# Preparing the next chunk six ticks earlier in a software-pipelined scan, with the logarithm's table change moved along

## The chip, the cores and the metric

One core of a Trainium2 chip runs the whole program in one launch. The metric is device time in microseconds of one execution; the profile is of one such execution. Engines are named as in the profile: PE is TensorE, DVE is VectorE, ACT is ScalarE, POOL is GpSimd, SP issues nearly all transfers.

## What is computed

Sixteen images of 64 channels and 64 x 64 pixels go through two layers (16 x 4096 positions each):

```python
# layer 0
y = leaky(conv3x3(x)); y = leaky(conv3x3(y)); seq = y as (image, 4096, 64)
x, z = split(seq @ in_proj)                       # 128 wide each
x = silu(causal_conv4(x) + b)
dt, B, C = split(x @ x_proj);  delta = softplus(dt @ dt_proj + dt_b)
h = exp(delta * A) * h + (delta * x) * B          # 4096 steps, 128 channels x 16 states
y = (h . C + x * D) * silu(z) @ out_proj
# layer 1, on y as (image, 64, 4096)
channel attention (64 x 64 softmax), spatial attention softmax(q^T k) (4096 x 4096), 1x1 conv, residual
```

softplus is done as max(t, 0) + ln(1 + exp(-|t|)) with a correction of the rounding of the sum, silu by the hyperbolic tangent; so ScalarE needs exp, tanh and ln.

## The kernel before

After the two convolutions (some 540 us), `pipeline` runs everything else as one software pipeline, written out by hand for each engine. Its unit is the *tick* T. An image has 128 ticks; 16 ticks (`GROUPS`) are a *chunk* of 512 positions. In each tick the scan handles one group of 8 channels x 16 states on 128 partitions: VectorE forms `DBU` (L1175, delta x u x B, into a bank) and runs the scan (L1189); ScalarE forms `dA` for the next tick (L1046, exp); GpSimd multiplies by C (L1317). In the same tick TensorE and the others do 1/128 of the attention of the image before: one difference product and one maximum product of the key search (L852, bank to `gains` by ScalarE L982, then VectorE's maximum L1127), four score products (L915, L917), ScalarE's two exponentials into `pr` (L1040), TensorE's products of the tick before with the values (L927) and, every second tick, with ones (L942). Image 0 has no attention beside it; behind the last scan tick, attention runs alone.

On top of that, once per chunk, come two chains, each step tied to r = T mod 16:

- the *preparing chain* of the chunk that comes next (`c = sl + 1`): r 0 `xin` and `z` products (L870), their copies, the first tap `cacc` (L1069); r 1 to 3 three taps on VectorE (L1219); r 4, 5 tanh (L1076, L1079); r 5, 6 gating into `u` and `zs` (L1229, L1234); r 6 the `dt` product (L874), its copy `dtx` (L1023), abs and exp (L1084, L1086), and the load of a later `seqt`; r 7 two VectorE steps; r 8 the logarithm (L1090); r 9 VectorE's `em1`, `dsp` (L1248, L1251) and GpSimd's `usp` (L1330); r 10 the stores of `dsp` and `usp` to `spread_d`, and the `BC` products (L878); r 11 the stores of `bcs`; r 12 the two broadcasts back, `bbc` and `cbc` (L724, L727).
- the *finishing chain* of the chunk that is done (`c = sl - 1`): r 2 the 32 products of `y` (L889), r 3 `ysb` (L1167, VectorE), r 4 the product with `zs` on GpSimd (L1323), r 7 `out` (L884), r 8 to 12 the split into three bfloat16 parts, r 12 `xv`, r 14 `en` and the stores of the parts.

Each engine runs its list in order and waits on semaphores. The SP queue is in order too: in each tick it fetches `lanes` for T + 3 (L736, 512 KB, four slots), behind whatever stores or loads its list has before. Every product uses the next of five banks of a ring (`RING`), and may start when the bank's use five before has been taken away by ScalarE or VectorE (`take_bank`). The order of the ring is the order of `plan` (L232). An `xin`, `z` or `dt` product shifts it by one.

ScalarE's tables: one table serves exp and tanh, another the logarithm. The compiler puts a table load in front of an activation that needs the other one, so twice a chunk.

Of the kernel before, what the change touches and what calls it, by code (L numbers as in the profile page):

```python
# [19 lines left out]
ALU = mybir.AluOpType  # L20
# [40 lines left out]
AHEAD = 3  # L61

# [41 lines left out]
class Span:  # L104
# [89 lines left out]
    def small_uses(self, T):  # L194
# [234 lines left out]
def pipeline(nc, banks, seq_d, scratch, w_in, cw, cb, w_dt_t, w_dt, dt_b, w_bc, a_log, skip,  # L429
# [4 lines left out]
    with ExitStack() as ctx:  # L434
        def sb(name, shape, dt=F32):
            return ctx.enter_context(nc.sbuf_tensor(name, shape, dt))
# [22 lines left out]
        u = sb("u", [P, 2, CHUNK])  # L459
# [22 lines left out]
        energy = sb("energy", [CH, CH])  # L482
# [12 lines left out]
        nmx = sb("nmx", [NT, 3, P])  # L495
        nm3 = sb("nm3", [NT, 3, P], BF16)
# [5 lines left out]
        catt = sb("catt", [CH, CH])  # L502
        cst1 = sb("cst1", [CH, 4])

# [14 lines left out]
        with nc.Block() as block:  # L519
            @block.vector  # L520
            def _(dve):
                nc.vector.memset(wxv[CH:P], 0.0)
                nc.vector.memset(mixw[:], 0.0)
                nc.vector.memset(ones[:], 1.0).then_inc(zeroed, 1)
# [48 lines left out]
        def span(j, images, tail, i):  # L573
# [22 lines left out]

            def bank_of(e):
                return RB[number[e] % RING]
# [16 lines left out]
            for T in range(sched.first, sched.last):  # L615
# [14 lines left out]
                c = sl + 1  # L630
# [7 lines left out]
                if r == 6 and sched.chunk(c + 2):  # L638
                    sched.note(f"seq{c % 2}", c + 2)
                elif T == sched.first == -GROUPS:  # L640
                    sched.note("seq0", 0)
                    sched.note("seq1", 1)
                c = sl - 1
# [26 lines left out]
            with nc.Block() as block:  # L670
                @block.sync
                def _(sp):
# [28 lines left out]
                    for T in range(first, last):  # L701
                        sl, r = T // GROUPS, T % GROUPS
                        c = sl + 1
# [34 lines left out]
                        c = sl - 1  # L738
# [96 lines left out]
                def _(pe):  # L835
# [6 lines left out]
                    def small_use(e):  # L842
# [29 lines left out]
                        elif kind == "dt":  # L872
                            wait(pe, "gated", c)
                            mm = nc.tensor.matmul(bank[:], wdt[:], u[:, c % 2, :], start=True, stop=True)  # L874
                        elif kind == "BC":
                            wait(pe, "gated", c)
                            for j in range(BLOCKS):
                                mm = nc.tensor.matmul(bank[BLOCK * j:BLOCK * (j + 1), 0:P], wbc[:],  # L878
                                                      u[:, c % 2, P * j:P * (j + 1)], start=True, stop=True,
# [92 lines left out]
                def _(act):  # L972
# [54 lines left out]
                    for T in range(first, last):  # L1027
# [36 lines left out]
                        c = sl + 1  # L1064
# [6 lines left out]
                        if sched.chunk(c) and r == 4:  # L1071
# [3 lines left out]
                            taken(act, ("y", c - 2))  # L1075
                            nc.scalar.activation(u[:, c % 2, :], cacc[:], ACT.Tanh).then_inc(S["tanh"], 1)  # L1076
# [14 lines left out]
                        c = sl - 1  # L1091
# [15 lines left out]
                def _(dve):  # L1107
# [52 lines left out]
                    for T in range(first, last):  # L1160
# [3 lines left out]
                        if sched.chunk(c) and r == 3:  # L1164
                            full_wait(dve, ("y", c))
                            full_wait(dve, ("out", c - 1))
                            nc.vector.scalar_tensor_tensor(out=ysb[:], in0=u[:, c % 2, :], scalar=dskip, in1=bank_of(("y", c))[:],  # L1167
# [38 lines left out]
                        c = sl + 1  # L1206
                        if sched.chunk(c):
# [18 lines left out]
                            if r == 5:  # L1226

                                wait(dve, "tanh", c)
                                nc.vector.scalar_tensor_tensor(out=u[:, c % 2, :], in0=u[:, c % 2, :], scalar=1.0,  # L1229
# [23 lines left out]
                        c = sl - 1  # L1253
# [46 lines left out]
                def _(pool):  # L1300
                    for T in range(first, last):
# [23 lines left out]
                        c = sl + 1  # L1325
                        if sched.chunk(c) and r == 9:
# [3 lines left out]
                            nc.gpsimd.tensor_tensor(usp[:], dsp[:], u[:, c % 2, :], ALU.mult).then_inc(S["du_in"], 1)  # L1330
# [44 lines left out]
```

## Time and profile before

| | us |
|---|---|
| three runs | 8232.38, 8223.09, 8398.1; median 8232.38 |
| the profiled execution | 8230.45 |
| its span, first to last instruction | 8228.7 |
| PE, DVE, ACT, POOL busy in the span | 7514.0 (91%), 6835.1 (83%), 5962.8 (72%), 3796.9 (46%) |
| first to last scan | 589 to 7820 |
| an inner chunk with attention (16 ticks) | 56.1 |

The page divides the span in 40 slices: from the fourth on TensorE is at 9 or 8 tenths nearly everywhere, VectorE at 8 or 9, and the DMA engines at 7 or 8 tenths with about 200 GB/s. The granted TensorE clock is full but for a few slices at the start (mean 0.966). So no engine stands out by its share alone, and what counts is the order of the work within a chunk. In the waits, idle time of an engine that isn't the bottleneck costs nothing: GpSimd's 2343 us of waiting for `DBU` is of that kind.

### The profile page before, as it was taken

To read this page: it belongs to the slowest core of one execution; us is meant where nothing else is said; L and a number is where in the kernel's file an instruction comes from. 1 tells how busy PE (TensorE), PEld (TensorE's weight loads), DVE (VectorE), ACT (ScalarE), POOL (GpSimd) and SP (SyncE) were. 2 spreads that over 40 slices of the span, in tenths; PEclk is the share of its full clock that TensorE was granted. 3 is DMA by queue.
4 is the path that set the end of the run, shared out by engine and by line. 5 is a ranking of instruction groups with operands and counts; after the bars stand their busy time and mean duration, and the time that the engine had idled before them with its cause. 6 is when DMAs were issued, how large, how long until landed. Compare 5 with 4: busy or idle time off the path is not lost. (4 is left out here: it accounts for less than half of the span.)

```text
span 8228.7 us, 151814 instructions
## 1 busy us (share of the span) xinstructions
PE 7514.0 (91%) x47106; PEld 2297.2 (28%) x47854; DVE 6835.1 (83%) x11132; ACT 5962.8 (72%) x10582; POOL 3796.9 (46%) x4135
## 2 busy tenths in 40 slices
PE   9962389999999999999989999999999999999998
PEld 2321122222222222222222222222222222222222
DVE  2228898898989889898888889888889898998876
ACT  1124577787878788787878788788878787887765
POOL 0016555555545455555545455555545454555500
PEclk9985699999999999999999999999999999999999
DMA  9838888888787788888877888888888878888710
GB/s 152 134 91 215 219 200 200 204 197 208 193 206 199 197 201 200 200 201 201 198 189 198 199 200 200 199 200 200 202 199 198 205 193 202 201 200 205 191 32 15
DMA packets 886523, 1530.96 MB, mean 186 GB/s; under 512 B 409480, under 2 KB 459472, under 8 KB 885712
## 3 DMA queue, kind: packets, MB, share of 16 engines
q1 hardware_dynamic: 882640, 1520.79, 76.7%
q8 instruction: 381, 6.24, 0.4%
q14 instruction: 430, 3.52, 0.2%
q10 hardware_dynamic: 3072, 0.40, 0.0%
HBM read 1326.69 MB, written 176.95 MB: 183 GB/s over the span
## 5 line engine op out<-in xcount | busy, mean ns | idle before, releaser
L1317 POOL TENSOR_TENSOR hst<-hst,cbc 128x512 f32<-128x512 f32 x2048 | 2620.2, 1279 | 2370.6 <-DVE bank L1175 2343.4
L1189 DVE TENSOR_TENSOR_SCAN hst<-dA,carry,bank 128x512 f32<-128x512 f32 x1792 | 2283.9, 1275 | 4.9 <-DVE bank L1175 0.4
L1040 ACT ACTIVATE pr<-bank 128x512 f32<-128x512 f32 x4096 | 2230.1, 604 | 43.2 <-PE bank L917 41.0
L927 PE MATMUL bank<-pr,vt 128*32 128x512 f32 x16384 | 2193.5, 608 | 0.7 <-ACT pr L1040 0.7
L982 ACT ACTIVATE gains<-bank 128x512 f32<-128x512 f32 x2048 | 1225.2, 598 | 832.7 <-PE bank L852 790.7
L1046 ACT ACTIVATE dA<-lanes,small 128x512 f32<-128x512 f32 x2048 | 1503.8, 734 | 431.8 <-DMA lanes<-spread_d 383.9
L852 PE MATMUL bank<-s1kx,s1q 128*128 128x512 bf16 x4096 | 1581.9, 387 | 133.0 <-DMA s1kx<-kx_d 84.9
L1127 DVE CUSTOM_DVE_ANT_0 gains<-bank,gains 128x512 f32<-128x512 f32 x2048 | 1404.3, 686 | 352.7 <-PE bank L852 333.9
L1175 DVE TENSOR_TENSOR bank<-lanes,bbc 128x512 f32<-128x512 f32 x2048 | 1505.0, 735 | 146.1 <-DMA lanes<-spread_d 65.0
L917 PE MATMUL bank<-t2q,t2k 128*128 128x512 bf16 x4096 | 1560.5, 381 | 46.6 <-DMA t2q<-nm 4.5
L915 PE MATMUL bank<-s1q,s1k 128*128 128x512 bf16 x3348 | 1278.6, 382 | 175.9 <-ACT pr L1040 152.6
L1310 POOL COPY carry<-hst 128x1 f32<-128x1 f32 x1792 | 815.1, 455 | 857.6 <-DVE hst L1189 856.0
L942 PE MATMUL bank<-pr,ones 128*32 128x512 f32 x7552 | 988.2, 595 | 2.4 <-ACT dens L1056 2.1
L852 PEld LDWEIGHTS bank<-s1kx,s1q 128*128 128x128 bf16 x4096 | 397.3, 97 | 1653.9 <-issue 714.0
L915 PEld LDWEIGHTS bank<-s1q,s1k 128*128 128x128 bf16 x4096 | 400.2, 98 | 715.5 <-ACT pr L1040 347.6
L927 PEld LDWEIGHTS bank<-pr,vt 128*32 128x32 f32 x16384 | 323.0, 108 | 826.1 <-issue 811.2
L889 PE MATMUL bank<-hst,cst 128*32 128x512 f32 x4096 | 480.6, 611 | 78.1 <-POOL hst L1317 78.1
L917 PEld LDWEIGHTS bank<-t2q,t2k 128*128 128x128 bf16 x4096 | 402.7, 98 | 400.9 <-issue 8.8
L398 ACT ACTIVATE biased<-bank,bias 128x512 f32<-128x512 f32 x128 | 81.1, 685 | 452.9 <-PE bank L386 443.0
L942 PEld LDWEIGHTS bank<-pr,ones 128*32 128x32 f32 x7552 | 245.3, 111 | 580.9 <-issue 414.2
L1330 POOL TENSOR_TENSOR usp<-dsp,u 128x512 f32<-128x512 f32 x128 | 213.1, 1664 | 260.4 <-DVE dsp L1251 260.4
L1167 DVE SCALAR_TENSOR_TENSOR ysb<-u,small,bank 128x512 f32<-128x512 f32 x128 | 95.6, 747 | 278.2 <-issue 268.8
(120 smaller groups left out, 5947.7 us busy)
## 6 DMA issues: line engine op xcount, KB each, us to landing
lanes<-spread_d SPq DMA_DIRECT2D x2048, 512.0 KB, 6.2
seqt<-seq_d SPq DMA_DIRECT2D x256, 128.0 KB, 4.7
spread_d<-dsp SPq DMA_DIRECT2D x128, 256.0 KB, 2.0
spread_d<-usp SPq DMA_DIRECT2D x128, 256.0 KB, 2.0
bbc<-bc_d SPq DMA_DIRECT2D x128, 256.0 KB, 4.3
cbc<-bc_d SPq DMA_DIRECT2D x128, 256.0 KB, 4.8
xpad<-in_x SPq DMA_DIRECT2D x64, 256.0 KB, 6.7
ypad<-ypad SPq DMA_DIRECT2D x128, 128.0 KB, 4.1
```

The source lines that it names most:

```text
L852: mm = nc.tensor.matmul(bank[:].rearrange("p (c n) -> p c n", n=HALF), s1q[:, q, nt * P:(nt + 1) * P], keys[:, 2 * mc:2 * (mc + 1), 1 if k ...
L915: nc.tensor.matmul(bank[:], s1k[:, t * P:(t + 1) * P], s1q[:, q, cols], start=True, stop=False)
L917: nc.tensor.matmul(bank[:], t2k[:, t * P:(t + 1) * P], t2q[:, q, cols], start=False, stop=True).then_inc(S["ring_full"], 1)
L927: mm = nc.tensor.matmul(ACC[CH * h + o:CH * h + o + BLOCK, :], vt[:, t, o:o + BLOCK], pr[:, T % PRING, h, :], start=t == 0, stop=t == KT - ...
L942: mm = nc.tensor.matmul(DEN[o:o + 32, :], ones[:], pr[:, (2 * p + par) % PRING, h, :], start=t == 1, stop=t == KT - 1, tile_position=(0, o))
L982: nc.scalar.activation(gains[:, k % 2, :], bank_of(e)[:], ACT.Relu).then_inc(S["act_took"], 1)
L1040: nc.scalar.activation(pr[:, T % PRING, h, :], bank_of(("S", T, h))[:], ACT.Exp).then_inc(S["p_full"], 1)
L1046: nc.scalar.activation(dA[:, (T + 1) % 2, :], lanes[:, (T + 1) % SLOTS, 0, :], ACT.Exp, scale=amat[:, g:g + 1]).then_inc(S["da_in"], 1)
L1127: nc.vector.tensor_tensor_reduce(out=gains[:, k % 2, :], in0=bank[:], in1=gains[:, k % 2, :], scale=1.0, scalar=LOWEST, op0=ALU.add, op1=A ...
L1175: nc.vector.tensor_tensor(DBU[:], lanes[:, T % SLOTS, 1, :], bbc[:, sl % 2, :], ALU.mult).then_inc(S["dbu_in"], 1)
L1189: nc.vector.tensor_tensor_scan(hst[:, slot_of(T), :], dA[:, T % 2, :], DBU[:], carry[:, g:g + 1] if sl % CHUNKS else 0.0, ALU.mult, ALU.ad ...
L1317: nc.gpsimd.tensor_tensor(h, h, cbc[:, (T - 1) // GROUPS % 2, :], ALU.mult).then_inc(S["hc_in"], 1)
```

## The change

`LEAD = 6` moves the whole preparing chain on every engine and in the SP queue: its tick is (T + 6) mod 16 and its chunk (T + 6) // 16 + 1. `xin` and `z` are thus in tick 10, the tanh in 14 and 15, `dt` and the exponential in tick 0, the logarithm in tick 2, `usp` in tick 3, the spread stores in 4, `BC` in 4, the `bcs` stores in 5, the broadcasts in 6, the `seqt` load in 0. The finishing chain stays. Since `u` now is written before the chunk two ahead of it is done with, it gets a third buffer. Behind the logarithm a one-column exponential of a spare tile is added. To make room, four small tiles of the attention are laid over the partitions of `rest` and `low` that the split leaves free.

```diff
+LEAD = 6
-        self.first = -GROUPS if j == 0 else 0
+        self.first = -GROUPS - LEAD if j == 0 else 0
...
-        for name in {0: ("xin", "z"), 6: ("dt",), 10: ("BC",)}.get(r, ()):
-            if self.chunk(sl + 1):
-                ev.append((name, sl + 1))
+        for name in {0: ("xin", "z"), 6: ("dt",), 10: ("BC",)}.get((T + LEAD) % GROUPS, ()):
+            c = (T + LEAD) // GROUPS + 1
+            if self.chunk(c):
+                ev.append((name, c))
...
-        u = sb("u", [P, 2, CHUNK])
+        u = sb("u", [P, 3, CHUNK])
...
+        nmx = rest[0:NT, 0:3 * P].rearrange("p (s n) -> p s n", n=P)
+        nm3 = low[0:NT, 0:3 * P].rearrange("p (s n) -> p s n", n=P)
+        energy = rest[0:CH, 3 * P:3 * P + CH]
+        catt = rest[0:CH, 3 * P + CH:4 * P]
...
+        spare = sb("spare", [P, 2])
...
+            def part_of(c):
+
+                return (c + CHUNKS * j) % 3
...
-                c = sl + 1
+                c, r = (T + LEAD) // GROUPS + 1, (T + LEAD) % GROUPS
...
-                            taken(act, ("y", c - 2))
-                            nc.scalar.activation(u[:, c % 2, :], cacc[:], ACT.Tanh).then_inc(S["tanh"], 1)
+                            taken(act, ("y", c - 3))
+                            nc.scalar.activation(u[:, part_of(c), :], cacc[:], ACT.Tanh).then_inc(S["tanh"], 1)
...
                             nc.scalar.activation(em1[:], em1[:], ACT.Ln).then_inc(S["ln_in"], 1)
-                        c = sl - 1
+                            nc.scalar.activation(spare[:, 1:2], spare[:, 0:1], ACT.Exp)
+                        c, r = sl - 1, T % GROUPS
```

The line with `(T + LEAD)` stands in the same way in the lists of SP, ScalarE, VectorE and GpSimd and in the counting of the semaphores; every other read of `u` changes to `part_of(c)`.

## Rows read from the trace of the kernel before

**Rows 1.** Stretches: length, busy PE, PEld, DVE, ACT, POOL, clock, DMA share, GB/s.

```profile
2102.30:2106.30 4.00, 4.00 (x30) 0.99 (x22) 2.99 (x6) 2.34 (x6) 2.35 (x3) 1.00 1.05 264
...
2109.50:2115.40 5.90, 5.85 (x52) 1.57 (x42) 3.83 (x7) 2.84 (x7) 1.95 (x3) 1.00 0.57 106
...
2118.50:2121.70 3.20, 3.20 (x23) 0.88 (x17) 3.10 (x5) 2.65 (x6) 3.09 (x4) 1.00 0.60 168
...
2134.50:2138.40 3.90, 2.59 (x18) 0.71 (x18) 3.79 (x7) 3.85 (x6) 2.02 (x2) 1.00 0.15 50
2138.40:2143.10 4.70, 4.65 (x38) 1.46 (x32) 4.60 (x7) 4.65 (x10) 3.06 (x5) 1.00 0.68 192
...
sum 56.10, PE 54.47 PEld 16.79 DVE 51.23 ACT 45.93 POOL 30.33; mean PE 3.40 PEld 1.05 DVE 3.20 ACT 2.87 POOL 1.90
```

**Rows 2.** The list of waits: us in total, times, longest.

```profile
DVE ysb L1167 <- issue: 268.8, 115, 4.5
...
PE bank L915 <- ACT pr L1040: 152.6, 117, 1.3
...
PE bank L852 <- DMA s1kx<-kx_d: 84.9, 15, 7.9
```

**Rows 3.** Grouped lines, whole trace: table loads (busy us, mean ns | idle before).

```profile
L1040 ACT ACT_TABLE_LOAD x117 | 150.1, 1283 | 2.1
```

**Rows 4.** Timeline, ticks 8 and 9: start, length, instruction [idle before].

```profile
4019.75 0.63 ACT L1090 ACTIVATE em<-em 128x512 f32<-128x512 f32 x1
...
4020.29 0.58 ACT L982 ACTIVATE gains<-bank 128x512 f32<-128x512 f32 x1
...
4020.88 1.28 ACT L1040 ACT_TABLE_LOAD   x1
...
4020.92 0.39 PE L915 MATMUL bank<-s1q,s1k 128*128 128x512 bf16 x1
...
4021.15 0.38 PE L917 MATMUL bank<-t2q,t2k 128*128 128x512 bf16 x1
...
4022.18 1.08 ACT L1040 ACTIVATE pr<-bank 128x512 f32<-128x512 f32 x2
...
4022.83 0.39 PE L915 MATMUL bank<-s1q,s1k 128*128 128x512 bf16 x1 [1.30 <-ACT pr L1040]
```

**Rows 5.** Timeline of ScalarE in tick 2 of another chunk.

```profile
2109.96 0.78 ACT L1046 ACTIVATE dA<-lanes,small 128x512 f32<-128x512 f32 x1
2113.80 0.60 ACT L982 ACTIVATE gains<-bank 128x512 f32<-128x512 f32 x1 [3.06 <-PE bank L852]
```

**Rows 6.** Timeline of TensorE in the same tick 2.

```profile
2109.76 3.62 PE L889 MATMUL bank<-hst,cst 128*32 128x512 f32 x32
...
2115.94 0.38 PE L915 MATMUL bank<-s1q,s1k 128*128 128x512 bf16 x1
```

**Rows 7.** Timeline of TensorE behind tick 0's `xin` and `z` products.

```profile
2104.23 0.39 PE L852 MATMUL bank<-s1kx,s1q 128*128 128x512 bf16 x1
...
2105.32 0.38 PE L852 MATMUL bank<-s1kx,s1q 128*128 128x512 bf16 x1
...
2106.62 0.39 PE L852 MATMUL bank<-s1kx,s1q 128*128 128x512 bf16 x1
```

**Rows 8.** Timeline behind tick 6's `dt` product, both engines.

```profile
4011.54 0.38 PE L852 MATMUL bank<-s1kx,s1q 128*128 128x512 bf16 x1
...
4013.72 0.58 ACT L982 ACTIVATE gains<-bank 128x512 f32<-128x512 f32 x1
...
4014.20 1.08 ACT L1040 ACTIVATE pr<-bank 128x512 f32<-128x512 f32 x2
```

**Rows 9.** Timeline of VectorE in tick 4.

```profile
2119.86 1.32 DVE L1175 TENSOR_TENSOR bank<-lanes,bbc 128x512 f32<-128x512 f32 x1
```

**Rows 10.** Timeline of the SP queue: `lanes` fetches behind the two broadcasts.

```profile
2146.62 1.18 SPq L736 DMA_DIRECT2D lanes<-spread_d  x2
```

**Rows 11.** Timeline of ScalarE: the `dA` of the first of these.

```profile
2152.66 0.72 ACT L1046 ACTIVATE dA<-lanes,small 128x512 f32<-128x512 f32 x1 [0.85 <-DMA lanes<-spread_d]
```

More of the change, by code:

```diff
@@ L523, in _ @@
                 nc.vector.memset(mixw[:], 0.0)
+                nc.vector.memset(spare[:], 0.0)
                 nc.vector.memset(ones[:], 1.0).then_inc(zeroed, 1)
@@ L639, in span @@
                     sched.note(f"seq{c % 2}", c + 2)
-                elif T == sched.first == -GROUPS:
+                elif T == sched.first and T < 0:
                     sched.note("seq0", 0)
                     sched.note("seq1", 1)
-                c = sl - 1
+                c, r = sl - 1, T % GROUPS
                 if sched.chunk(c):
@@ L701, in _ @@
                     for T in range(first, last):
-                        sl, r = T // GROUPS, T % GROUPS
-                        c = sl + 1
+                        c, r = (T + LEAD) // GROUPS + 1, (T + LEAD) % GROUPS
                         if r == 6 and sched.chunk(c + 2):
@@ L737, in _ @@
                                                 near.partition_broadcast(D_STATE)), f"lanes{X % SLOTS}")
-                        c = sl - 1
+                        c, r = T // GROUPS - 1, T % GROUPS
                         if sched.chunk(c):
@@ L873, in small_use @@
                             wait(pe, "gated", c)
-                            mm = nc.tensor.matmul(bank[:], wdt[:], u[:, c % 2, :], start=True, stop=True)
+                            mm = nc.tensor.matmul(bank[:], wdt[:], u[:, part_of(c), :], start=True, stop=True)
                         elif kind == "BC":
@@ L878, in small_use @@
                                 mm = nc.tensor.matmul(bank[BLOCK * j:BLOCK * (j + 1), 0:P], wbc[:],
-                                                      u[:, c % 2, P * j:P * (j + 1)], start=True, stop=True,
+                                                      u[:, part_of(c), P * j:P * (j + 1)], start=True, stop=True,
                                                       tile_position=(0, BLOCK * j))
@@ L1166, in _ @@
                             full_wait(dve, ("out", c - 1))
-                            nc.vector.scalar_tensor_tensor(out=ysb[:], in0=u[:, c % 2, :], scalar=dskip, in1=bank_of(("y", c))[:],
+                            nc.vector.scalar_tensor_tensor(out=ysb[:], in0=u[:, part_of(c), :], scalar=dskip, in1=bank_of(("y", c))[:],
                                                            op0=ALU.mult, op1=ALU.add).then_inc(S["dve_took"], 1)
@@ L1205, in _ @@
                                                     ALU.add).then_inc(S["gathered"], 1)
-                        c = sl + 1
+                        c, r = (T + LEAD) // GROUPS + 1, (T + LEAD) % GROUPS
                         if sched.chunk(c):
@@ L1228, in _ @@
                                 wait(dve, "tanh", c)
-                                nc.vector.scalar_tensor_tensor(out=u[:, c % 2, :], in0=u[:, c % 2, :], scalar=1.0,
+                                nc.vector.scalar_tensor_tensor(out=u[:, part_of(c), :], in0=u[:, part_of(c), :], scalar=1.0,
                                                                in1=cacc[:], op0=ALU.add,
@@ L1252, in _ @@
                                                                op0=ALU.max, op1=ALU.add).then_inc(S["delta_in"], 1)
-                        c = sl - 1
+                        c, r = sl - 1, T % GROUPS
                         if sched.chunk(c) and r == 8:
@@ L1324, in _ @@
                                 S["y2_in"], 1)
-                        c = sl + 1
+                        c, r = (T + LEAD) // GROUPS + 1, (T + LEAD) % GROUPS
                         if sched.chunk(c) and r == 9:
@@ L1329, in _ @@
                             wait(pool, "st_sp", c - 1, 32)
-                            nc.gpsimd.tensor_tensor(usp[:], dsp[:], u[:, c % 2, :], ALU.mult).then_inc(S["du_in"], 1)
+                            nc.gpsimd.tensor_tensor(usp[:], dsp[:], u[:, part_of(c), :], ALU.mult).then_inc(S["du_in"], 1)
             clear(nc, list(S.values()))
```

8 lines of the change are left out of this document (2 added, 6 removed).

## The prediction

> **What bounds the kernel now.** I read the busy table by stretches first [rows 1]. It cuts one chunk in the middle of an image into its ticks, a tick being the time from one scan's start to the next. All 16 ticks take 56.10 us; TensorE is busy for 54.47 of them, VectorE for 51.23, ScalarE for 45.93. So TensorE is the bound, with 1.63 us of idle time per chunk, and the reader should look for where that lies: in tick 9 TensorE works 2.59 of 3.90 us (1.31 idle), while the others shown (ticks 0, 2, 4 and 10) are full. The list of waits [rows 2] names the cause: TensorE's first score product waits for ScalarE's `pr` 152.6 us in all, 117 times, 1.3 us each, once in nearly every one of the 120 chunks that have attention beside the scan (15 of 16 images, 8 chunks each). The grouped lines [rows 3] show 117 activation table loads at the softmax exponential L1040, each 1283 ns: the same count and the same length. The timeline of ticks 8 and 9 [rows 4] puts them in order: the chunk's logarithm has replaced the exponential's table, `gains` is copied, then the table comes back (4020.88, 1.28 us) while a full bank of scores waits; `pr` starts at 4022.18 and TensorE's next product at 4022.83.
>
> What the wait costs TensorE: the product before began at 4021.15, and the one before that at 4020.92, a pitch of 0.23; the late one came 1.68 later, so 1.45 is lost. The same two ticks hold a smaller wait of that first product for `gains` (it starts at 4020.92, just behind the end of `gains` at 4020.87), so that I put the loss at 1.6 us per chunk, between the 1.45 and the 1.63 of all idle time in [rows 1].
>
> **The change part by part.**
>
> *Nothing is taken out of the chunk's work.* Every product, tap, copy and transfer of the preparing chain stays and moves from ticks 0 to 12 to ticks 10 to 15 and 0 to 6. VectorE keeps its 51.23 us a chunk, under any period that I forecast, so it isn't the bound on average.
>
> *The table reloads.* The logarithm moves from tick 8 to tick 2, the `y` products' tick, and a one-column exponential behind it brings the table back there. In that tick ScalarE ends `dA` at 2110.74 (2109.96 + 0.78) and waits until 2113.80, 3.06 us, since TensorE is in its 32 products of `y` (3.62 us) [rows 5, 6]. Into this gap go a load (1.28), the logarithm (0.63), a load (1.28) and the one-column exponential, which I put at 0.2 (bounds 0.1 and 0.6; the 128x512 logarithm of [rows 4] is its ceiling): 3.4 us. ScalarE is 0.3 us late at `gains`. The first product that needs this `gains` starts at 2115.94 [rows 6], 2.1 us after 2113.80, and `gains` takes 0.6, so the lateness is covered: cost 0. Without that cover it would be 0.3 x 120 = 40 us. The gain is the 1.6 us in tick 9, which then has no load: 1.6 x 117 = -187 us; lower bound, by the loads alone, 1.28 x 117 = -150.
>
> The Trainium skill, "ScalarE: Activation LUTs", section "What ACT_TABLE_LOAD costs", speaks against this: it gives a switch 1.28 us of load and about 1.38 us of drain, 2.66 together, so by it the block in tick 2 would be near 6 us and not fit. The trace disagrees: between the end of `gains` at 4020.87 and `pr` at 4022.18 lie 1.31 us, the load alone [rows 4].
>
> *The `dt` product and its three activations move from tick 6 to tick 0*, in the place of the `xin`/`z` products, which go to tick 10. The tick behind tick 0 is a short one for TensorE: 2104.23 to 2106.62, 2.39 us, from one difference product to the next [rows 7]. The tick behind tick 6 is longer, as it has the `out` product. After `dt` [rows 8], counted from the difference product at 4011.54, `gains` ends 2.76 later (4013.72 + 0.58) and the two `pr` 3.74 later (4014.20 + 1.08). In a 2.39 us tick the last product of the next tick stands at 2.39 + 1.09 = 3.48 (1.09 is 2105.32 less 2104.23 in [rows 7]) and needs the bank of the second `pr`: 0.3 us late, a new wait of TensorE in tick 1 or 2. 0.33 x 120 = +40 us. Bounds: 0 (if the scores come round earlier) and 0.6 (70 us).
>
> *`xin`/`z` in tick 10.* TensorE's work there grows by what tick 0 loses, ScalarE gets two copies and the first tap. Tick 10 already holds VectorE's long subtraction, 4.70 us of tick with VectorE at 4.60 [rows 1]. TensorE's own need in tick 10 is then that of tick 0 now, about 4.3, so the three engines need about the same there and none waits long for another: 0, at most 0.3 a chunk.
>
> *VectorE's and GpSimd's operations.* One tap leaves tick 2, where VectorE had it under the `y` wait (its `ysb` waited 268.8 us, 115 times, 2.3 each [rows 2]); it costs its length elsewhere, but against TensorE's period this is free. Ticks 3 and 4 get crowded: the two last subtractions, then `usp` on GpSimd directly ahead of `ysb` in tick 4. VectorE's `DBU` product in tick 4, with `ysb` on GpSimd, took 1.32 us [rows 9]; I put half of that down to the meeting, and count two such meetings instead of one, 0.6 us more of VectorE. It falls behind TensorE by up to 1.8 us there, and catches up in ticks 5 to 9, which have lost their extra operations. Cost 0; if the banks run out, 0.3 a chunk.
>
> *The SP queue.* The two spread stores with their waits for `dsp` and `usp` now stand in tick 4, the four `bcs` stores in tick 5, the two broadcasts in tick 6, each in front of a `lanes` fetch. Today the fetch behind the broadcasts goes out at 2146.62, 8.2 us behind scan 10 (2138.40), and the `dA` that needs it starts at 2152.66 having waited 0.85 [rows 10, 11], 14.3 behind scan 10; nobody on TensorE's path waits for it, since tick 14 is long. Moved, it serves tick 9. Scan 4 to scan 9 is 16.0 us now (2118.50 to 2134.50 [rows 1]); the operations that leave ticks 5 to 7 take, by my estimate, 1.6 of it, and tick 9's `DBU` starts two VectorE operations of 0.65 ahead of its scan: 13.1 us. But the `BC` copy comes some 2 us earlier in its tick, and fewer bytes stand in the queue: landing 12 to 14.3. I take 0.1 us a chunk, +12 us; bounds 0 and 1.2 (14.3 less 13.1), 144 us.
>
> *Transfers at the image's start.* TensorE waits 84.9 us, 15 times, for the keys `s1kx` [rows 2]; the 0.5 MB of broadcasts leave the queue ahead of the splits that these depend on, the 0.25 MB of `seqt` (tick 0) come into it. At the 264 GB/s of the busiest tick [rows 1] that is 1 us net, x 15 = -15 us; bounds -42 (half of the wait) and +15.
>
> *Ramp, third `u` buffer, shared tiles:* six more ticks in front without scan, 0 to 6 us once, I take 3. The third buffer and the tiles laid over `rest` and `low` use partitions that those leave free: 0.
>
> Sum: -187 + 40 + 12 - 15 + 3 = -147 us. The profiled execution took 8230.45 (span 8228.7), 2 under the median of 8232.38. 8230 - 147 = 8083, and on the median 8085. As a share this is 1.8%.
>
> **The rivals.**
>
> 1. *Everything comes and no new wait.* If the scores come round early enough behind `dt`, its 40 us vanish, and a lighter queue takes 5 us more of the key wait: 8232 - 187 - 15 - 5 = 8025. For it: ScalarE has 10 us of spare time a chunk [rows 1]. Against: the bank order in a 2.39 us tick is strict. Chance 0.2.
> 2. *The wait moves.* `lanes` of tick 9 land late, or VectorE stands too far behind in ticks 4 to 6 for TensorE to find a bank: 0.7 us a chunk more than the sum, 84 us: 8085 + 84 = 8169. It decides once landing is over 13.1 us behind scan 4. For it: the `dA` of the same fetch already waits 0.85 today [rows 11]. Chance 0.2.
> 3. *The change doesn't do what it says:* the two loads stay apart, or tick 9 is held by something else (VectorE's tick 9 was full as well, 3.8 of 3.9). But its two subtractions leave that tick too. 8225 to 8250. Chance 0.06.
> 4. *Slower.* Each switch holds ScalarE for two load lengths when logarithm and exponential stand directly together: 4 x 1.28 + 0.63 + 0.2 = 6.0 us in a gap of 3.06, 2.9 late, 1.5 of it covered (2.1 - 0.6), 1.4 x 120 = 170 on the sum: 8255. It decides from 1.3 us more per chunk. (It is the Trainium skill's drain, page and section as above; the trace, as said, has no such gap.) Chance 0.04.
>
> **How the numbers follow.** Forecast 8085, chance 0.5, its own range 8055 to 8120 (the 70 and 0 us of the new wait, the 150 of the gain). Rival 1 reaches down to 8010, rival 2 up to 8230. The range 8020 to 8175 leaves out about 0.2: the upper part of rival 2, rivals 3 and 4, and the lowest of rival 1. Within 2% is about what a measurement of this kernel can tell from no change; 2% below is 8068. Faster by more: all of rival 1 and a fourth of the forecast's case, 0.33. Slower by over 2% would need 8397: 0.01. The rest, 0.66, is within.
>
> **What would show it.** Right: the 117 loads at L1040 are gone and stand at the new exponential, none at `dA`; the wait of L915 for `pr` falls from 152.6 to under 40 us; tick 9 comes to about 2.7 us; a small new wait for `gains` or `pr` behind tick 1 of about 0.3 x 120; VectorE's idle time in tick 2 grows by a tap. Wrong: tick 2 longer than 5.9 us (the block doesn't fit), `DBU` or `dA` waiting for `lanes` in ticks 7 to 9 (the queue), VectorE-bound ticks 3 to 6, or a key wait well above 84.9 us.

## The result, and the profile after

The changed kernel takes 8565.51 us (median of four runs), the kernel before beside it on the same chip 8229.52: the ratio is 1.041, with a 95% interval of 1.0386 to 1.0433. It is 4% slower, where 1.8% faster was forecast, and outside the range. Three of the four runs took 8562.22 to 8567.01; the fourth, at a mean granted clock of 0.562, took 14671.15 and, like the 8398.1 among the runs of before, is a slow run that the ratios leave out. The profiled execution took 8564.01, its span is 8562.2.

The engines' line of the page of the changed kernel (busy us, share of the span, instructions):

```profile
PE 7630.7 (89%) x47106; PEld 2307.1 (27%) x47854; DVE 6877.0 (80%) x11133; ACT 6012.7 (70%) x10710; POOL 3736.5 (44%) x4135
```

Lines of the changed kernel lie 7 or 8 below those of before: L859 is the difference product (L852 before), L922 and L924 the scores, L1047 `pr`, L1053 `dA`, L989 `gains`, L1183 `DBU`, L1197 the scan, L743 the `lanes` fetch, L717 and L720 the spread stores, L726 the `bcs` stores, L731 and L734 the broadcasts, L704 the query load.

**What came as forecast.** First the table loads. In the grouped lines of the changed kernel (busy us, mean ns | idle before) all 256 loads of the chunks stand at the logarithm and at the one-column exponential behind it; `pr` has none, where [rows 3] had 117:

```profile
L1097 ACT ACT_TABLE_LOAD x128 | 164.2, 1283 | 2.3
L1098 ACT ACT_TABLE_LOAD x128 | 164.2, 1283 | 2.3
```

And in the timeline of ScalarE (start, length, instruction), tick 2 of a chunk of the changed kernel, they lie in the gap that [rows 5] showed:

```profile
2209.16 0.75 ACT L1053 ACTIVATE dA<-lanes,small 128x512 f32<-128x512 f32 x1
2209.94 1.28 ACT L1097 ACT_TABLE_LOAD   x1
2211.23 0.63 ACT L1097 ACTIVATE em<-em 128x512 f32<-128x512 f32 x1
2211.88 1.28 ACT L1098 ACT_TABLE_LOAD   x1
2213.17 0.20 ACT L1098 ACTIVATE spare<-spare 128x1 f32<-128x1 f32 x1
2213.39 0.60 ACT L989 ACTIVATE gains<-bank 128x512 f32<-128x512 f32 x1
```

The block from 2209.94 to 2213.39 is 3.45 us, against 3.4 in the working, and `gains` starts with no idle time in front of it. The list of waits has no wait of a score product for `pr` any more, and in the even chunks tick 9 takes 2.60 us on average, where it took 3.90 and 2.7 was forecast.

**What came instead.** The list of waits of the changed kernel (us in total, times, longest):

```profile
ACT dA L1053 <- DMA lanes<-spread_d: 780.6, 508, 6.8
...
PE bank L859 <- DMA t2q<-parts_d: 211.4, 45, 9.8
DVE bank L1183 <- DMA lanes<-spread_d: 171.3, 130, 6.1
...
PE bank L859 <- DMA s1kx<-kx_d: 74.9, 15, 5.9
...
PE bank L859 <- ACT xin L1032: 58.1, 58, 2.2
```

Before, `dA` waited 383.9 us for `lanes` (283 times) and `DBU` 65.0 (48 times), and the wait for the queries (`t2q<-parts_d`) came once, 1.6 us. The queries are loaded once in two chunks, in the odd ones (counted from 0 in each image). `DBU` now waits 130 times, about once in each of the 128 chunks; the query wait comes 45 times, and 45 is 3 of the 8 chunks of each of 15 images. To see where in a chunk this falls, I cut one of these chunks into its ticks again. The table of stretches (length, then busy PE, PEld, DVE, ACT, POOL, granted clock, DMA share, GB/s), ticks 4 and 6 to 9 of a chunk of the changed kernel:

```profile
2218.74:2221.92 3.18, 3.13 (x21) 1.06 (x19) 3.08 (x5) 2.44 (x5) 3.10 (x4) 1.00 0.38 139
...
2225.09:2227.68 2.59, 2.59 (x14) 0.74 (x13) 2.49 (x5) 1.36 (x3) 1.14 (x3) 1.00 0.78 215
2227.68:2230.28 2.60, 2.60 (x19) 0.70 (x21) 2.50 (x5) 2.60 (x6) 1.76 (x3) 1.00 0.62 179
2230.28:2236.32 6.04, 3.30 (x25) 0.70 (x18) 3.02 (x6) 2.18 (x5) 1.85 (x3) 1.00 1.03 230
2236.32:2243.42 7.10, 3.67 (x14) 1.09 (x18) 2.86 (x8) 4.89 (x9) 2.21 (x3) 0.52 1.04 248
```

Ticks 4, 6 and 7 are full. Ticks 8 and 9 take 13.14 us, and TensorE works 6.97 of them. This is an odd chunk and a long one: over the odd chunks 3, 5 and 7 of the images 1 to 15 the two ticks take 11.3 us on average, where they took 7.5 before. Tick 8 ends with a wait for `lanes`, tick 9 holds one for the queries. The timelines of VectorE and then TensorE (in brackets the idle time before and what ended it):

```profile
2234.97 0.70 DVE L1183 TENSOR_TENSOR bank<-lanes,bbc 128x512 f32<-128x512 f32 x1 [2.96 <-DMA lanes<-spread_d]
...
2239.75 0.58 PE L859 MATMUL bank<-s1kx,s1q 128*128 128x512 bf16 x1 [6.13 <-DMA t2q<-parts_d]
2240.13 0.63 PE L922 MATMUL bank<-s1q,s1k 128*128 128x512 bf16 x1
```

Both transfers were late because they were issued late. The timeline of the SP queue over the same time:

```profile
2217.64 0.35 SPq L717 DMA_DIRECT2D spread_d<-dsp  x1
2219.38 0.35 SPq L720 DMA_DIRECT2D spread_d<-usp  x1
2219.84 1.84 SPq L743 DMA_DIRECT2D lanes<-spread_d  x1
2221.79 1.91 SPq L726 DMA_DIRECT2D bc_d<-bcs  x4
2223.82 0.52 SPq L743 DMA_DIRECT2D lanes<-spread_d  x1
2227.40 0.52 SPq L731 DMA_DIRECT2D bbc<-bc_d  x1
...
2228.67 1.17 SPq L743 DMA_DIRECT2D lanes<-spread_d  x2
2229.93 2.28 SPq L704 DMA_DIRECT2D s1q<-parts_d  x4
2232.26 1.02 SPq L704 DMA_DIRECT2D t2q<-parts_d  x2
```

SP works through a list in order. It stands at the top of this one until `dsp` is there (2217.64; 8.5 us of waiting), then for `usp`, from 2217.99 to 2219.38, and then for the landing of the `bcs` stores, which the broadcasts read back: from 2224.34 to 2227.40. The `lanes` of ticks 9 and 10 go out at 2228.67, 9.9 us behind scan 4 (2218.74), and land at 2234.97. The query load stands behind them. The waits of the SP queue in the changed kernel:

```profile
SPq L717 <- DVE dsp L1259: 894.6, 128, 14.7
SPq L731 <- DMA bc_d<-bcs: 327.4, 128, 3.8
...
SPq L720 <- POOL usp L1338: 175.5, 128, 1.4
```

In the kernel before, the query load came in time for its use. Its timeline, SP and then TensorE:

```profile
4010.83 1.93 SPq L696 DMA_DIRECT2D s1q<-parts_d  x4
4012.80 0.89 SPq L696 DMA_DIRECT2D t2q<-parts_d  x2
...
4020.53 0.39 PE L852 MATMUL bank<-s1kx,s1q 128*128 128x512 bf16 x1
```

There 6.8 us lie between the end of the last issue (4013.69) and the first product that needs the new queries. In the changed kernel the last issue ends at 2233.28 and the product starts 6.5 us later, nearly all of it spent waiting.

The load also took longer. The list of DMA issues (KB each, median us from issue to landing), before and then changed:

```profile
t2q<-parts_d SPq DMA_DIRECT2D x128, 64.0 KB, 3.4
...
t2q<-parts_d SPq DMA_DIRECT2D x128, 64.0 KB, 6.1
```

So before there were some 3.4 us in reserve (6.8 - 3.4). In the changed kernel the last issue ends 13.1 us behind scan 4 on average (chunks 1, 3 and 5 of the images 1 to 15), where it was 9.5, and the load then needs 2.7 us more to land.

**The sum over the kernel.** Means over the images 1 to 15, from the starts of the scans in the timelines (even: chunks 2, 4 and 6; odd: chunks 3 and 5): a chunk took 56.2 (even) and 56.0 us (odd) before and takes 56.6 and 61.6; chunk 7 went from 56.9 to 62.6, chunk 1 from 63.7 to 68.6, chunk 0 from 55.8 to 56.3. That is 3 x 0.3 + 3 x 5.6 + 4.9 + 0.5 = 23.1 us an image, x 15 = 347; image 0, which has no attention, is 6 us shorter (380.7 to 374.5). 347 - 6 = 341, against the 336 of the medians. The loss lies in the odd chunks.

### The profile page after: what moved, and what is told of

It is laid out like the page before. It is cut to its first block and busy times, and to the rows that moved or that the text cites. A ratio compares the mean times of both kernels' runs of the same rounds, so it can differ in the third digit from the quotient of the medians.

```text
span 8562.2 us, 151944 instructions
## 1 busy us (share of the span) xinstructions
PE 7630.7 (89%) x47106; PEld 2307.1 (27%) x47854; DVE 6877.0 (80%) x11133; ACT 6012.7 (70%) x10710; POOL 3736.5 (44%) x4135
## 5 line engine op out<-in xcount | busy, mean ns | idle before, releaser
L1197 DVE TENSOR_TENSOR_SCAN hst<-dA,carry,bank 128x512 f32<-128x512 f32 x1792 | 2285.4, 1275 | 6.8 <-ACT dA L1053 1.5
L1047 ACT ACTIVATE pr<-bank 128x512 f32<-128x512 f32 x4096 | 2231.7, 603 | 65.4 <-PE bank L924 64.6
L934 PE MATMUL bank<-pr,vt 128*32 128x512 f32 x16384 | 2233.3, 618 | 0.7 <-ACT pr L1047 0.7
L1053 ACT ACTIVATE dA<-lanes,small 128x512 f32<-128x512 f32 x2048 | 1500.8, 733 | 827.8 <-DMA lanes<-spread_d 780.6
L859 PE MATMUL bank<-s1kx,s1q 128*128 128x512 bf16 x4096 | 1609.2, 394 | 453.5 <-DMA t2q<-parts_d 211.4
L1183 DVE TENSOR_TENSOR bank<-lanes,bbc 128x512 f32<-128x512 f32 x2048 | 1536.4, 750 | 255.2 <-DMA lanes<-spread_d 171.3
L924 PE MATMUL bank<-t2q,t2k 128*128 128x512 bf16 x4096 | 1588.6, 388 | 80.1 <-issue 25.6
L989 ACT ACTIVATE gains<-bank 128x512 f32<-128x512 f32 x2048 | 1220.3, 596 | 594.5 <-PE bank L859 454.9
L922 PE MATMUL bank<-s1q,s1k 128*128 128x512 bf16 x3348 | 1305.3, 390 | 46.2 <-ACT gains L989 45.9
L1318 POOL COPY carry<-hst 128x1 f32<-128x1 f32 x1792 | 704.6, 393 | 1014.8 <-DVE hst L1197 1013.6
L859 PEld LDWEIGHTS bank<-s1kx,s1q 128*128 128x128 bf16 x4096 | 400.4, 98 | 2019.5 <-issue 1237.9
L922 PEld LDWEIGHTS bank<-s1q,s1k 128*128 128x128 bf16 x4096 | 403.7, 99 | 610.8 <-ACT pr L1047 168.3
L924 PEld LDWEIGHTS bank<-t2q,t2k 128*128 128x128 bf16 x4096 | 408.2, 100 | 422.0 <-issue 37.7
```

What stands on the lines that cost most here:

```text
L859: mm = nc.tensor.matmul(bank[:].rearrange("p (c n) -> p c n", n=HALF), s1q[:, q, nt * P:(nt + 1) * P], keys[:, 2 * mc:2 * (mc + 1), 1 if k ...
L922: nc.tensor.matmul(bank[:], s1k[:, t * P:(t + 1) * P], s1q[:, q, cols], start=True, stop=False)
L924: nc.tensor.matmul(bank[:], t2k[:, t * P:(t + 1) * P], t2q[:, q, cols], start=False, stop=True).then_inc(S["ring_full"], 1)
L934: mm = nc.tensor.matmul(ACC[CH * h + o:CH * h + o + BLOCK, :], vt[:, t, o:o + BLOCK], pr[:, T % PRING, h, :], start=t == 0, stop=t == KT - ...
L989: nc.scalar.activation(gains[:, k % 2, :], bank_of(e)[:], ACT.Relu).then_inc(S["act_took"], 1)
L1047: nc.scalar.activation(pr[:, T % PRING, h, :], bank_of(("S", T, h))[:], ACT.Exp).then_inc(S["p_full"], 1)
```

## The experiments

Two parts of the changed kernel's SP list can be at fault: the spread stores, `bcs` stores and broadcasts with their waits, which the change puts in front of the fetches of ticks 7 to 9, and the place of the query load behind them. Beside this the prediction's gain, the table loads, had to be sized by itself. All ratios are to the kernel before, on the same chip.

**The query load alone.** Five ticks earlier in SP's list (tick 2 instead of 7), in front of the stores:

```diff
-QUERY_LOAD = SEARCH - 3
+QUERY_LOAD = SEARCH - 8
```

> The changed kernel with the load of the queries (s1q, t2q) five ticks earlier in the list of SP, in tick 2 instead of 7, ahead of the spread stores and broadcasts that the change put into ticks 4 to 6. Theory Q, that the odd chunks' 5.3 us more are the late query load: the wait of TensorE for t2q (211.4 us, 45 times) vanishes, odd chunks come from 61.7 to about 57, 60 x 5 = 300 us less: 8270. Theory L, that the lanes fetch for tick 9 and all that waits in it does it, and the query load is only seen last: the load gone, lanes still come late, ticks 8 to 11 stay long, 8450 to 8560.

Measured 8278.29 us, 1.0056 [1.0041, 1.0071]. The wait for `t2q` is gone from the list and odd chunks take 56.6 instead of 61.6 us. That returns 287 us. The waits of the difference product for the queries in the changed kernel were 211.4, in the chunks 1, 3 and 5; at the same place in chunk 7 of 14 images it waited 62.4 more, to which the profile gives no releaser. These are gone too, and the sum is 273.8. The waits for `lanes` stay (764.6 for `dA`, 163.8 for `DBU`), and with them a kernel that is no faster than before.

The same edit in the kernel before is the control:

> Control: the kernel before with its query load in tick 2 instead of 7, nothing else. There the load is in time, so moving it gives nothing: 8225 within 25. If it is faster by more, the gain of this edit in the changed kernel is not its stall alone.

Measured 8228.71, 1.0004 [0.9994, 1.0013]: there the query load was not late, so an earlier one gives nothing.

**The stores and broadcasts later, and nothing else.** They aren't needed before the next chunk. In this order, the spread stores go from tick 4 to 6, the `bcs` stores from 5 to 7, the broadcasts from 6 to 9 (`r` is counted in the chain's own ticks, six ahead); the query load stays where it was:

```diff
-                        if sched.chunk(c) and r == 10:
+                        if sched.chunk(c) and r == 12:
-                        if sched.chunk(c) and r == 11:
+                        if sched.chunk(c) and r == 13:
-                        if sched.chunk(c) and r == 12:
+                        if sched.chunk(c) and r == 15:
```

> The same later stores with the query load left where the change has it, tick 7. If the query load is late because SP stands at the usp wait, the stores and the broadcast's round trip ahead of it, it goes out some 4 us earlier now and nearly all of the odd chunks' stall goes: at most 60 us over the run with both. If it is late by its place and the length of the DMA queue alone, the stall stays above 3 us in 60 chunks: 200 us or more over the run with both.

Measured 8010.81 us (8009.94 to 8014.6), 0.9742 [0.9726, 0.9758]: 2.6% faster than before and 555 us faster than the change as it was made (549 by the two ratios). From here on this kernel is called the fast version. Its list of waits:

```profile
ACT dA L1053 <- DMA lanes<-spread_d: 101.3, 81, 7.3
```

`DBU` waits 8.5 us for `lanes` (6 times), the difference product 3.0 for the queries (once). In the SP queue's list hardly anything is left of the waits for `dsp` (12.1 us, once) and for the `bcs` landing (4.5 us, 4 times), and that for `usp` is gone; what it waits for is now the slot that a fetch needs:

```profile
SPq L594 <- DVE bank L1183: 2799.3, 1170, 11.1
```

Its timeline over the ticks 4 to 8 of a chunk (scan 4 at 2110.52) shows no hole at the broadcasts or at `usp` in front of the query load:

```profile
2110.65 0.58 SPq L717 DMA_DIRECT2D spread_d<-dsp  x1
2111.29 0.42 SPq L720 DMA_DIRECT2D spread_d<-usp  x1
2113.28 0.52 SPq L743 DMA_DIRECT2D lanes<-spread_d  x1
2113.92 3.26 SPq L726 DMA_DIRECT2D bc_d<-bcs  x4
2117.29 0.54 SPq L743 DMA_DIRECT2D lanes<-spread_d  x1
2117.93 1.92 SPq L704 DMA_DIRECT2D s1q<-parts_d  x4
2119.89 0.89 SPq L704 DMA_DIRECT2D t2q<-parts_d  x2
...
2122.15 0.55 SPq L731 DMA_DIRECT2D bbc<-bc_d  x1
```

SP's list runs ahead of the scans as far as free slots let it. So the spread stores, two places later in the list, still go out right at scan 4 (2110.65), and now find their operands ready; in the places of the change SP stood there waiting for `dsp`, about 7 us a chunk (894.6 / 128), and lost its lead. The query load's issue ends at 2120.78, 10.3 us behind scan 4; in the changed kernel it ended 14.5 behind (2233.28 - 2218.74). It lands in 3.5 us (median), against 6.1. The stretches of ticks 8 and 9 here:

```profile
2122.06:2125.17 3.11, 3.06 (x21) 0.66 (x14) 3.02 (x8) 2.32 (x5) 1.85 (x3) 1.00 1.05 233
2125.17:2128.06 2.89, 2.89 (x26) 0.92 (x22) 2.75 (x7) 2.82 (x6) 1.63 (x3) 1.00 1.08 291
```

6.00 us in place of 13.14, with TensorE busy throughout and the DMA share as high as in the late ticks: it was not bandwidth.

Both edits together:

> The changed kernel with the query load in tick 2 and, in the list of SP alone, the spread stores two ticks later (tick 6), the bcs stores two later (7) and the broadcasts three later (9), so that SP finds dsp, usp and bcs ready and the lanes fetches of ticks 7 to 9 aren't held. Theory L, that the 1.8 us which TensorE still loses in ticks 10 and 11 with the query load early come from ScalarE waiting for these lanes (764.6 us of waits in that run): the wait falls to about the 384 us of before or less, DBU's wait to under 70, ticks 8 to 11 lose 1.5 us, 8278 - 1.5 x 120 = about 8100. Theory A, that ScalarE is simply too full in ticks 9 to 12 (head, two copies, a tap, mid beside its own): lanes come in time and the chunk stays at 56.5, 8240 to 8280.

Measured 8012.85, 0.9744 [0.973, 0.9759]: the same. Once the list isn't held, the place of the query load is worth nothing.

**Which of the holds.** Only the broadcasts go back by three ticks; the waits for `dsp` and `usp` stay:

```diff
-                        if sched.chunk(c) and r == 12:
+                        if sched.chunk(c) and r == 15:
```

> The changed kernel with only the two broadcasts (bbc, cbc) issued three ticks later; the stores of dsp and usp and the four of bcs stay where the change put them. Theory R (the round trip of bcs holds the list: SP's 327.4 us of waits for the landing of the four stores of bcs, behind which stand the fetches of ticks 8 and 9 and the query load): nearly all of the loss goes, 8020 to 8080. Theory S (the waits for dsp and usp hold it: 894.6 and 175.5 us): those waits are left as they are, and so is most of the time, 8400 to 8550. A share for each would lie between, about 8200.

Measured 8118.05, 0.9871 [0.9857, 0.9886]. SP's wait for the landing of `bcs` is gone (1.1 us). So, taken in this order, this hold, 327.4 us in SP's list, is worth 447 of the 555 us; the other 107 come with the holds for `dsp` and `usp`, 1070 us in the same list, and the later `bcs` stores. That the 0.5 MB of broadcasts left the place ahead of the fetches isn't what helped: `lanes` and the queries take as long to land as before this edit (7.2 and 6.1 us; 6.8 and 6.1). The queries' last issue ends 9.5 us behind scan 4 on average, instead of 13.1. Neither of the two pure theories came out; the first was near. The list of this kernel:

```profile
SPq L717 <- DVE dsp L1259: 915.6, 128, 16.6
...
SPq L720 <- POOL usp L1338: 175.6, 128, 1.4
```

The longest wait in total costs less. My reading, which no run shows by itself, is that what stands right behind it (the `lanes` of tick 7) has its reserve, and the shorter one comes when the reserve is used up. What the first still costs shows in the queries: with the issue as early as in the fast version (9.5 us), they take 6.1 us to land instead of 3.5, and the difference product waits for them 50.0 us, 42 times.

**The control of that.** In the kernel before, the same three entries one tick later (one tick is the room there is):

```diff
-                        if sched.chunk(c) and r == 10:
+                        if sched.chunk(c) and r == 11:
-                        if sched.chunk(c) and r == 11:
+                        if sched.chunk(c) and r == 12:
-                        if sched.chunk(c) and r == 12:
+                        if sched.chunk(c) and r == 13:
```

> Control: the kernel before with the stores of dsp and usp, of bcs and the broadcasts each one tick later in SP's list, the chain itself unmoved. In the kernel before SP waits 577.4 us for dsp too. If later places are worth something by themselves, without the chain's shift, this gives part of the 214 us that they gave beyond the kernel before in the changed one: 8100 to 8180. If they only matter because of the shift: 8225 within 20. One tick is all the room there is in front of the first fetch of the next chunk, and a late landing of its rows could cost up to 50.

Measured 8169.46, 0.9936 [0.9922, 0.9951]: 53 us faster: later places are worth something by themselves, at the low end of what was expected of that. `dA` waits for `lanes` 118.7 us instead of 383.9. Inner chunks are as long as before (56.1, 56.0); chunk 1 of an image fell from 63.7 to 60.8, image 0 from 380.7 to 370.1.

**The table loads by themselves.** In the kernel before, an exponential in the place of the logarithm (the logarithm is left out), so that no table changes:

```diff
-                            nc.scalar.activation(em1[:], em1[:], ACT.Ln).then_inc(S["ln_in"], 1)
+                            nc.scalar.activation(em1[:], em1[:], ACT.Exp).then_inc(S["ln_in"], 1)
```

> The kernel before, with the logarithm computed as an exponential (so this leaves the logarithm out and the output is another one): no table load is left in the chunk, at the same place and with the same list of work. It measures what was at stake in tick 9. If TensorE's 1.6 us of idle time per chunk come from the load alone, as I forecast: 8230 - 1.6 x 117 = 8043, within 20, and the wait of TensorE for pr at the first score product falls from 152.6 us to under 20. If the transfers or VectorE hold the chunk anyway (rival: the bound is elsewhere), 8180 to 8230.

Measured 8100.37, 0.9843 [0.9827, 0.986]: 125 us, two thirds of the 187 that the prediction booked. The wait of L915 for `pr` is gone, and others have grown:

```profile
ACT dA L1046 <- DMA lanes<-spread_d: 485.5, 367, 12.7
...
DVE bank L1175 <- DMA lanes<-spread_d: 72.2, 64, 11.4
PE bank L852 <- DVE mxp L1127: 50.3, 74, 2.4
```

The difference product now waits 50.3 us for VectorE's maximum (18.8 before), so VectorE ends part of the wait that ScalarE ended. By ticks the gain isn't where it was booked: in the even chunks tick 9 goes only from 3.90 to 3.71 us, of which, in one of these chunks (2116.31 to 2120.02), VectorE is busy for 3.68 and TensorE now for all 3.71. What TensorE gets done there it saves later: tick 14 goes from 3.79 to 2.76.

The same edit in the fast version (and no callback):

> The same kernel with an exponential in the place of the logarithm and no callback, so that no table changes: it leaves the logarithm out, and its output is not the reference's. It gives what the two table loads of a chunk still cost. In the kernel before this edit gave 125 us. If the shift has put the loads beside other work, as the forecast had it, the time is 8011 less no more than 30. If they still stand in the way, 7890 to 7950.

Measured 8015.64, 0.9746 [0.973, 0.9762]; with both tables it was 8010.81. In tick 2 the 256 loads cost nothing that can be measured. This is the step of the prediction on which its gain rested, and it holds.

**The callback by itself.** In the kernel before, the one-column exponential behind the logarithm in tick 8:

```diff
                             nc.scalar.activation(em1[:], em1[:], ACT.Ln).then_inc(S["ln_in"], 1)
+                            nc.scalar.activation(cst1[:, 3:4], ones[0:CH, 0:1], ACT.Exp)
```

> The kernel before with the one-column exponential behind the logarithm alone, nothing moved. The load then stands in front of the gains copy of tick 9 instead of behind it. My account of the table (it holds ScalarE 1.28 us wherever it stands, and ScalarE has no gap in ticks 8 and 9): same time within 30 us, TensorE waits for gains instead of pr, about 1.3 x 117 in sum, plus 0.2 us x 128 for the added instruction = +25 at most. Rival, that calling the table back alone is worth something as TensorE had the scores already: 20 to 60 us faster. Rival, that it costs more: gains late delays the maximum too: 8300.

Measured 8235.35, 1.0013 [1.0003, 1.0022]: the load only changes its place in the same two ticks, and TensorE's first score product waits for `gains` (197.9 us, 22.1 before) instead of `pr`. The changed kernel without the callback:

```diff
-                            nc.scalar.activation(spare[:, 1:2], spare[:, 0:1], ACT.Exp)
```

> The changed kernel without the added exponential: the table comes back with the first softmax exponential behind the y products, 1.28 us later than ScalarE could have had it. If the callback in the y gap does what I counted: 1.28 us of ScalarE in tick 3 that is no longer covered, of which the first product that needs gains and pr leaves 0 to 1 us to TensorE: 0 to 120 us slower than the changed kernel, 8565 to 8685. If the slowdown came from the added instruction or its load: faster than 8565.

Measured 8554.35, 1.0395 [1.038, 1.0411], against 1.041 [1.0386, 1.0433] with it: the same. A callback that did its work would have made the kernel without it slower, by up to 120 us; the 11 us that its median is lower are inside the intervals. And the fast version without it:

> The changed kernel with the stores two ticks later (8010.8) without the one-column exponential behind the logarithm, so that the table load falls to the next exponential that is needed. Theory C (moving the load is worth something once SP's list holds nothing up): slower than 8010.8 by about one table load on the path for most chunks, 128 x 1.283 x 0.3 to 0.7, so 8060 to 8125. Theory D (after the shift the logarithm stands where the engine has room behind it anyway): 8011 within 15.

Measured 8018.22, 0.9751 [0.9736, 0.9766], 7 us more than with it, inside the intervals. Of the change's two means for the tables only the shift of the logarithm does anything; the callback is worth at most these few us.

**Do the gains add up?** The kernel before with its stores one tick later and without the logarithm (which is left out):

```diff
-                        if sched.chunk(c) and r == 10:
+                        if sched.chunk(c) and r == 11:
...
-                            nc.scalar.activation(em1[:], em1[:], ACT.Ln).then_inc(S["ln_in"], 1)
+                            nc.scalar.activation(em1[:], em1[:], ACT.Exp).then_inc(S["ln_in"], 1)
```

> The kernel before with the stores and broadcasts one tick later and an exponential in the place of the logarithm (it leaves the logarithm out, and its output is not the reference's). By itself the one edit gave 53 us and the other 125. If the two are separate losses of the kernel before, this is at 8222 - 53 - 125 = 8044 within 20, and what the changed kernel with its stores two ticks later has beyond it (8011) is of the size of what image 0 became shorter (33 us). If both remove one and the same wait, the time stays near the better of the two, 8090 to 8110.

Measured 8059.77, 0.9796 [0.978, 0.9813]: 167 us, near the sum of 178 and away from the better of the two. The table wait and the held list are separate losses of the kernel before. Inner chunks take 55.1 and 54.5 us here and 54.7 and 54.8 in the fast version: no difference on average. Most of the 49 us that the fast version has beyond this one lies at the edges: image 0 takes 347.2 instead of 369.4 us (22), and chunk 1 of an image 61.2 instead of 62.6 (1.4 x 15 = 21).

## Why the prediction was wrong

**The gain: mechanism right, term too large.** The loads lie where the prediction put them, the block takes 3.45 us for a forecast 3.4, the one-column exponential 0.20 as estimated, `gains` is not late, and with the list free the loads cost nothing. The Trainium skill's rule of a drain beside each switch ("ScalarE: Activation LUTs", "What ACT_TABLE_LOAD costs") is not what this trace shows: with two switches in a row, instruction follows load at 2211.23 and 2213.17, 1.29 behind each load's start. Rival 4 is out. But the term of -187 us was 1.6 us a chunk, more than the 1.30 of the wait itself (152.6 in all), as if nothing else stood right behind it. The loads taken away by themselves gave 125. The prediction had noted that VectorE was full in tick 9, 3.79 of 3.90 [rows 1], and dismissed it, since two of its subtractions leave that tick with the shift. That argument bears on the shifted kernel: in the fast version tick 9 of the even chunks takes 2.60 us, and the inner chunks are about 1.5 (even) and 1.2 us (odd) shorter than before.

**The wait behind tick 0: +40 us, part of it came, and the time didn't grow.** The working has a slip: 3.74 - 3.48 is 0.26 us, not 0.33, so 31 us. A new wait of this size is there: the score products of L924 wait 25.3 us for `gains`, 97 times, nearly all in tick 1, and none did before (the 45.9 of L922 lie in other ticks). But ticks 0 and 1 together take 7.04 us where they took 7.24 (even chunks), so the lower bound, 0, is what came of it. The two meetings of VectorE and GpSimd (1.28 and 1.27 us at `DBU`, in ticks 4 and 5) cost nothing, as worked out: ticks 4 to 7 are full. Tick 10 with `xin` and `z` was put at 0 and wasn't free: TensorE waits there for ScalarE's copy `xin`, 58.1 us in 58 even chunks. In the fast version this wait is gone, so it belongs to the cost of the late `lanes`, which ScalarE waits for, and not to a tick that is too full. The keys' wait fell by 10 us for a forecast 15.

**The SP queue: the step that failed.** It priced one entry, the fetch behind the broadcasts, at +12 us with an upper bound of 144. By its own rule (landing over 13.1 us behind scan 4 decides) the trace says where it lies: issued 9.9 us behind scan 4, landed 16.2 behind (2234.97 - 2218.74), and `DBU` waited 2.96. The waits for `lanes` in ticks 7 to 9 were also among its own signs of being wrong. The working had 8.2 for the issue from [rows 10] and took it to come earlier after the move, 12 to 14.3 for the landing; it came later. In its new place the `bcs` stores took longer to come back: their last issue ended at 2223.70 and the broadcast went out at 2227.40, 3.7 us, where before it was 2.35 (2143.00 to 2145.35). Rival 2 had the place and the condition right and its price wrong: 0.7 us a chunk, where even chunks lose 1.9 against the fast version (56.6 - 54.7), in ticks 8, 10 and 14.

What is larger was not in the working at all: **the query load**. It stands in tick 7, behind the fetches that the broadcasts hold, and tick 9's difference products need it. In the odd chunks it costs 5.0 us more (61.6 - 56.6). The prediction counted the queue's entries that the change moves and the one fetch behind them, and did not go down the list to everything else behind the holds, with the reserve of each. The chunk of [rows 1] is an even one, which has no query load. What was needed stood in the trace of before: 6.8 us from the last issue to the first use, and 3.4 to land, so 3.4 in reserve. In the changed kernel the load goes out 3.5 us later on average by the holds (13.1 behind scan 4, against 9.5 in the fast version; 14.5 against 10.3 in the chunks shown), which uses up the reserve, and it takes 6.1 to land where 3.4 was usual, since SP, once released, issues several large fetches right in front of it. That last cause is my reading; the fetches stand there in SP's timeline, and the landing is 3.5 in the fast version, where they don't.

So the sum, by what the runs showed: where the forecast had -187 for the tables, the one measured alone was -125; where it had +12 for the queue, the queue cost 555 against the same kernel with its stores later. That version, at 8010.8, lies 14 us under the rival without any new wait (8025). This is luck in part: rival 1 leaves out the +12 and +3 of the prediction's own sum, with which it would be 8040, and the later stores also free the list of a hold that the kernel before had itself (53 us), which makes up for the smaller gain from the tables.

**Open.** The split of the queue's loss between `usp`'s and `dsp`'s waits wasn't tried. Why image 0 gains more with the shift (347.2) than with later stores alone (370.1) wasn't looked at further than that it does.

## What to carry to other kernels

When a step is moved in an engine's or queue's written order, list every entry that then stands behind its waits, down to the next point where the queue has caught up, and set against each its reserve: from last issue to first use in the trace, less the time to land, with room for a slower landing (3.4 us became 6.1 here). A store that waits for a fresh result, and above all a load that waits for a store to land, is worth trying later in a prefetching queue, up to what its consumer allows, and not only where its operand becomes ready: here 2 to 3 places decided between 4% slower and 2.6% faster. A wait on the bounding engine can be worth less than its length, where another engine's wait stands right behind it; taking the cause out by itself (125 for a booked 187) is the way to size it.

## What the hardware showed beside this

TensorE's granted clock fell in the stall. It had stood idle for 6.13 us before 2239.75; the granted clock is 1.00 in the stretch from 2232.60 to 2234.60 and 0.50, the 1.2 GHz level, from 2236.60 to 2238.60, with TensorE idle. In the stretch from 2236.32 to 2243.42 it is 0.52, and 1.00 in the ticks around. The products behind the stall took 0.63 us where they take 0.38; they run until the `ones` product at 2243.75, which is at full pace again:

```profile
2242.40 1.53 PE L934 MATMUL bank<-pr,vt 128*32 128x512 f32 x8
2243.75 1.03 PE L949 MATMUL bank<-pr,ones 128*32 128x512 f32 x8
```

The same sequence of products at full clock, elsewhere in the changed kernel:

```profile
2189.70 0.38 PE L859 MATMUL bank<-s1kx,s1q 128*128 128x512 bf16 x1
...
2191.08 1.07 PE L934 MATMUL bank<-pr,vt 128*32 128x512 f32 x8
```

From the first difference product to the `pr` products it is 1.38 us here and 2.65 behind the stall (2239.75 to 2242.40), and the `pr` products themselves take 1.35 to the `ones` products instead of 0.88 (2186.85 to 2187.73 in the chunk before). So the stall cost about 1.7 us beyond its 6.13. The mean granted clock of the span went from 0.966 to 0.948. From 962 us to the last scan the clock's records have it at the lower level 79 times, 512 us in sum, against 21 times and 171 us before; 55 of the 79 are at tick 9 of an odd chunk. With the query load early it is 24 times and 191 us. How much of the 555 us is this was not separated: the waits for the queries alone sum to 273.8, and the earlier query load returned 287.
